# Local attention: one output product a step, with the three value terms added on GpSimd and VectorE

## The reference, cut to what matters

```python
q = (x @ WQ_w + WQ_b).reshape(Bx, Lx, nh, d)
k = (x @ WK_w + WK_b).reshape(Bx, Lx, nh, d)
ak = (ax @ WK_w + WK_b).reshape(Bx, 1, nh, d)
av = (ax @ WV_w + WV_b).reshape(Bx, 1, nh, d)
pad_k = jnp.pad(k, ((0, 0), (1, 1), (0, 0), (0, 0)))
k_shift = jnp.stack([pad_k[:, t:Lx + t] for t in range(3)], axis=3)
...
K = jnp.concatenate([akb, k_shift], axis=3)
V = jnp.concatenate([avb, k_shift], axis=3)
scores = jnp.einsum('blhd,blhjd->blhj', q, K) / jnp.sqrt(jnp.float32(d))
alphas = jax.nn.softmax(scores, axis=-1)
att = jnp.einsum('blhj,blhjd->blhd', alphas, V).reshape(Bx, Lx, nh * d)
return att @ WO_w + WO_b
```

## Time and profile before

| | us |
|---|---|
| median of 3 runs | 1583.0 |
| lowest and highest of them | 1581.71, 1587.13 |
| the profiled execution, its own time | 1581.07 |
| span of its trace | 1579.0 |
| TensorE busy, whole span | 1460.8 (93%) |
| VectorE busy | 732.8 (46%) |
| ScalarE busy | 651.0 (41%) |
| GpSimd busy | 106.7 (7%) |

### The profile page before, as it was taken

One profiled execution on the slowest core, in us unless ns is written; L12 is line 12 of the kernel. 1 busy time (PEld: TensorE's weight loads), 2 busy tenths in 40 slices (PEclk: granted clock), 3 DMA queues, 4 the chain that ended last, 5 costly groups with the idle time before them and its releaser, 6 DMA issues. The chain is left out here.

```text
span 1579.0 us, 30235 instructions
## 1 busy us (share of the span) xinstructions
PE 1460.8 (93%) x11078; PEld 1132.5 (72%) x11078; DVE 732.8 (46%) x2721; ACT 651.0 (41%) x2429; POOL 106.7 (7%) x141
## 2 busy tenths in 40 slices
PE   7999978999989999999999998799999999767995
PEld 5333324777779999999999996488888888644663
DVE  3576765455433444444444445633333332863223
ACT  2322204565524554554554552134444443622442
POOL 4000000000000000000000000100000000004662
PEclk8999989999999999999999998599999999957998
DMA  5000000000030000000000000100000000001113
GB/s 158 1 0 0 1 0 1 1 1 1 1 108 1 1 2 2 1 2 1 2 1 2 1 2 1 34 21 22 22 22 28 22 2 1 1 27 33 42 43 96
DMA packets 27724, 27.95 MB, mean 18 GB/s; under 512 B 2293, under 2 KB 22234, under 8 KB 27450
## 3 DMA queue, kind: packets, MB, share of 16 engines
q1 hardware_dynamic: 20970, 16.70, 3.6%
q0 software_dynamic: 2496, 5.12, 1.1%
q10 hardware_dynamic: 4112, 4.19, 0.9%
HBM read 21.35 MB, written 4.65 MB: 16 GB/s over the span
## 5 line engine op out<-in xcount | busy, mean ns | idle before, releaser
L1625 PE MATMUL spare<-identb 128*128 128x128 bf16 x3166 | 218.4, 219 | 0.0
L1625 PEld LDWEIGHTS spare<-identb 128*128 128x128 bf16 x3166 | 202.0, 103 | 4.3
L1223 DVE TENSOR_TENSOR_SCAN narg<-rz,pre_n 128x16 f32<-128x16 f32 x256 | 47.9, 187 | 220.2 <-PE pre_n L1120 219.0
L1158 ACT ACTIVATE ghid<-gh_ps,cols 128x128 f32<-128x128 f32 x512 | 144.3, 365 | 12.9 <-PE gh_ps L1059 12.7
L1059 PE MATMUL gh_ps<-hist,w 128*128 128x128 f32 x1024 | 137.5, 275 | 0.6 <-ACT ghid L1158 0.6
L1068 PE MATMUL gy_ps<-w2e,ghid 128*128 128x128 f32 x1024 | 136.8, 276 | 0.8 <-DVE g_diff L1204 0.3
L1068 PEld LDWEIGHTS gy_ps<-w2e,ghid 128*128 128x128 f32 x1024 | 124.4, 191 | 3.2 <-issue 3.2
L1059 PEld LDWEIGHTS gh_ps<-hist,w 128*128 128x128 f32 x1024 | 125.9, 188 | 0.8 <-DVE hist L1231 0.8
L1144 ACT ACTIVATE rz<-pre_r 128x8 f32<-128x8 f32 x256 | 45.6, 178 | 181.9 <-PE pre_r L1120 179.2
L1120 PE MATMUL pre_r<-hist,gru_w 128*128 128x128 f32 x512 | 118.1, 311 | 0.8 <-DVE hist L1231 0.5
L1676 DVE TENSOR_TENSOR_SCAN targ<-gates,pairs 128x16 f32<-128x16 f32 x256 | 49.1, 192 | 140.8 <-ACT gates L1635 140.8
(11 more groups left out here) (412 smaller groups left out, 2516.4 us busy)
## 6 DMA issues: line engine op xcount, KB each, us to landing
w<-in_L_ffn_W SPq DMA_DIRECT2D x1, 2048.0 KB, 9.6
raw<-in_L_ffn_wg SPq DMA_DIRECT2D x8, 256.0 KB, 3.0
raw<-in_L_ffn_wu SPq DMA_DIRECT2D x8, 256.0 KB, 2.8
raw<-in_L_ffn_wd SPq DMA_DIRECT2D x8, 256.0 KB, 2.7
wqkv<-in_L_attn_Wqkv SPq DMA_DIRECT2D x1, 1536.0 KB, 6.6
mrow<-mt SPq DMA_DIRECT2D x4, 256.0 KB, 2.4
y_top<-yrow SPq DMA_DIRECT2D x4, 256.0 KB, 5.4
y_next<-yrow ACTq DMA_DIRECT2D x4, 256.0 KB, 5.8
```

What stands on the lines that cost most here:

```text
L1158: nc.scalar.activation(hid[v % 2][:, f, :], h_ps[:, f, :], ACT.Relu, bias=n.cols[:, at:at + 1]).then_inc(h_done, 1)
L1223: V.tensor_tensor_scan(narg[p][:, :], rz[p][:, 0:16], n_slot(s), 0.0, ALU.mult, ALU.add).then_inc(narg_done, 1)
L1625: nc.tensor.matmul(spare[:, 0:P], n.identb[:, :], n.identb[:, :], start=True, stop=True)
```

## The change

The third term is no longer a product of its own: it is added to the pair sum, and one product with the sum of all three is left. The first addition moves from VectorE to GpSimd, and VectorE adds the third term one step later, between `weighted(u, 0)` and `weighted(u, 1)` of the next unit. A semaphore `all_done` is new. TensorE waits for it ahead of `project_out`. The number of additions on VectorE stays 32.

```diff
@@ block.gpsimd
+                def pair_terms(u):
+                    if not 0 <= u < STEPS:
+                        return
+                    pool.wait_ge(term_done, J * u + 2)
+                    if u >= 2:
+                        pool.wait_ge(y_part, u - 1)
+                    nc.gpsimd.tensor_tensor(pair[u % 2][:, :], term[u % 2][:, 0, :], term[u % 2][:, 1, :],
+                                            ALU.add).then_inc(pair_done, 1)
+
+                for u in range(STEPS):
+                    pair_terms(u)
@@ block.tensor, project_out
-                    pe.wait_ge(term_done, J * (u + 1))
-                    nc.tensor.matmul(y_ps[:, :], wo[:, c, :], term[u % 2][:, J - 1, :], start=False, stop=False)
-                    pe.wait_ge(pair_done, u + 1)
+                    pe.wait_ge(all_done, u + 1)
                     nc.tensor.matmul(y_ps[:, :], wo[:, c, :], pair[u % 2][:, :], start=False,
                                      stop=(c == NC - 1)).then_inc(y_part, 1)
@@ block.vector
                     if u >= 2 and j == 0:
-                        dve.wait_ge(y_part, u - 1)
+                        dve.wait_ge(pair_done, u - 1)
+                        dve.wait_ge(all_done, u - 1)
...
-                def pair_terms(u):
+                def all_terms(u):
                     if not 0 <= u < STEPS:
                         return
-                    dve.wait_ge(term_done, J * u + 2)
-                    nc.vector.tensor_tensor(pair[u % 2][:, :], term[u % 2][:, 0, :], term[u % 2][:, 1, :],
-                                            ALU.add).then_inc(pair_done, 1)
+                    dve.wait_ge(pair_done, u + 1)
+                    dve.wait_ge(term_done, J * (u + 1))
+                    nc.vector.tensor_tensor(pair[u % 2][:, :], pair[u % 2][:, :], term[u % 2][:, J - 1, :],
+                                            ALU.add).then_inc(all_done, 1)
...
                     weighted(u, 0)
+                    all_terms(u - 1)
                     if split:
                         soft_reciprocal(g)
                     weighted(u, 1)
...
                     if g is not None and at == 0:
                         soft_shift(g)
-                    pair_terms(u)
                     if split:
```

More of the change, by code:

```diff
@@ L232, in local_attention @@
         parts_done = sem("parts_done"); turned = sem("turned"); turned_kept = sem("turned_kept"); p0_kept = sem("p0_kept")
-        spread = sem("spread"); term_done = sem("term_done"); pair_done = sem("pair_done")
+        spread = sem("spread"); term_done = sem("term_done"); pair_done = sem("pair_done"); all_done = sem("all_done")
         y_part = sem("y_part"); y_kept = sem("y_kept")
```

## The result

The changed kernel took 1596.97 us in the median of 7 runs (1593.45 to 1603.44), the kernel before 1579.52 on the same chip (7 runs, 1575.41 to 1587.13). The ratio is 1.0109, with a 95% interval of 1.0081 to 1.0138: slower by about 17 us. The forecast was 1580.6, with a range from 1573 to 1587; it started from a median of 3 runs of the kernel before, 1583.0, that has become 1579.5 with 7, so its miss in the difference (2.4 less forecast, 17 more measured) is larger than the two times show. The profiled execution took 1594.89 us, its span is 1593.1.

What follows compares the result with a forecast made beforehand. TensorE set the 5.38 us step, the keys' ring limiting it to 5.12. Gains 6.4, less 1.9 (last steps) and 2.1 (softmax collisions), made 2.4 us less: 1583.0 to 1580.6 us, range 1573 to 1587.

Steps and rivals of the forecast that it cites:

- the nine steps of units 20 to 22 and 26 to 31: Steps without key projections and three-tap products: 3.43 us each against 3.22, 0.21 more each, a loss of 1.9 us.
- the ring: Last steps: third term, first term, second addition, product, third spread, back to third term; 3.43 us against 3.22.
- the 0.9 of the last group's first unit: Last group, where no keys and no product follow: the removed product's whole 0.86 us gained once.
- The clock rival: After each softmax TensorE idles 0.7 longer, 3.4 us more at 1.2 GHz: +5 us, 1585.7; 10 in 100.
- the 0.26 of unit 19: Unit 19, one of seven steady steps: each shrinks from 5.38 to 5.12 us, a gain of 0.26.
- The softmax collision: Steps 17, 25, 33: GpSimd's addition runs behind the three-tap product and delays VectorE's difference 0.7 each, 2.1 us lost.
- the steady step: Mid-group steps, units 3 to 5, 11 to 13 and 19: from 5.38 to 5.12 us, 1.8 us gained.
- the keys' ring: Third term, ScalarE's key copy, key projection, spread, second term, three-tap product, third term: 5.12 us, a step's lower limit.
- the addition's ring: Steady step: output product to next first term, second addition, back to the product; 5.09 us, just below 5.12.
- GpSimd's 1.28 alone: GpSimd's first addition: 1.28 us in the last steps, over 2 us where it lies behind a three-tap product.
- the rival at 1607: GpSimd takes the port ahead of the three-tap product in 20 steps, 1.2 us more each: +24 us; 10 in 100.
- the one at 1566: Keys' ring has slack and TensorE keeps the pace: some 20 steps gain 0.86 each, 17 us; 7 in 100.

Runs made afterwards that it cites:

- e2: Changed kernel plus one useless fp32 matmul of 512 columns a unit in units 20 to 31; 1585.2 us, ratio 1.0051 to the kernel before.
- e1: Kernel before with its third output product left out and nothing else changed; 1584.56 us, ratio 1.0027 to the kernel before.
- e4: Kernel before with its one addition moved to GpSimd and both output products kept; 1586.01 us, ratio 1.0035 to the kernel before.
- e8: Changed kernel with GpSimd held in units 7, 15 and 23 until the softmax's last cast; 1590.5 us, ratio 1.0060 to the kernel before.
- e9: The hybrid with a key ring of 13 slots instead of 12; 1573.29 us, ratio 0.9954 to the kernel before.
- the hybrid: Changed kernel in units 0 to 19, GpSimd held in units 7 and 15; two products and VectorE's old addition from unit 20; 1579.97 us, ratio 0.9977.
- e11: The hybrid without the hold on GpSimd in units 7 and 15; 1583.7 us, ratio 1.0013 to the kernel before.
- e7: Changed kernel plus one useless matmul of 256 columns a unit in units 20 to 31; 1587.2 us, ratio 1.0029 to the kernel before.
- e3: Changed kernel with the first addition back on VectorE in its old place; 1600.18 us, ratio 1.0131 to the kernel before.
- e10: e9 with the second addition moved ahead of the next unit's first term; 1571.21 us, ratio 0.9937 to the kernel before.
- e6: Changed kernel plus one useless matmul of 512 columns a unit in units 24 to 31 only; 1589.07 us, ratio 1.0042 to the kernel before.

## Why the prediction was wrong, by its steps

**The step that failed** is "I price the nine steps of units 20 to 22 and 26 to 31 with that, 0.21 each": 3.43 us a step, a loss of 1.9 us. The length was worked out at the 2.4 GHz level from rows of the kernel before, and the change took away what kept that level. In units 26 to 31 the step was 4.6 us. The excess of 1.17 is all in TensorE's two links of the ring: product to spreading 2.01 instead of 1.07, spreading to third term 0.65 instead of 0.41. With the clock brought back (e2) the same step is 3.42, so the ring was right and its clock was not. From unit 23 to the end of the stage that is +10.8 us, where the forecast has 6 x 0.21 = 1.3 less the 0.9 of the last group's first unit, so +0.4; the 1.8 us behind the stage come on top. e1 shows that one product a step less is enough for the loss, without the new waits. What I should have asked of the rows: TensorE is busy only 14.90 of 18 us in these steps before the change, the clock stood at 0.69 right behind a softmax with TensorE idle in it, and the change takes 0.86 us of work out of each of these steps with nothing to fill its place. I took the 1.00 of the row over as if it belonged to the place and not to the work.

**The clock rival** asked about the wrong place. It had 3.4 us more of the low level after each softmax, +5 us. That did happen after the second softmax (6.8 us instead of 3.4), but the large piece is that the clock did not return after the last one.

**Units 20 to 22** were mis-sized for a reason of their own, and the clock has no part in it: from unit 18 to 22 it was +2.96 instead of 3 x 0.21 = 0.6 less the 0.26 of unit 19, and e2, with the clock at 1.00 up to 209.9, takes the same 18.16 us. In steps 29 and 30 VectorE is the bound: the three-tap product, three terms and an addition are 1.67 + 4 x 0.61 = 4.11, and the step was 4.15 and 4.13. The product that closes a unit waits for that line. In step 33 the product of unit 22 stands behind the sum of the exponentials on VectorE as well, and TensorE waited 2.19 us for it. The rows of the changed kernel:

```profile
194.93 1.12 PE L411 MATMUL y_ps<-pair,wo 128*128 128x512 f32 x2 [0.86 <-DVE pair L654]
...
199.06 1.13 PE L411 MATMUL y_ps<-pair,wo 128*128 128x512 f32 x2 [0.88 <-DVE pair L654]
...
203.22 1.12 PE L411 MATMUL y_ps<-pair,wo 128*128 128x512 f32 x2 [1.17 <-DVE pair L654]
...
208.95 2.08 PE L411 MATMUL y_ps<-pair,wo 128*128 128x512 f32 x2 [2.19 <-DVE pair L654]
```

**The softmax collision** was taken as 0.7 "by the order of starts", with 0 and 1.28 as bounds. It is the upper bound's mechanism: GpSimd starts 0.03 after L612 and 0.24 ahead of the product, and the product is 1.08 longer. The order of starts was misread: the term ends at 112.47 and the product starts at 112.78, because two short operations stand between them, so by that order GpSimd comes first. In the steady step nothing stands between, and the product was ahead (89.22 against 89.38). In the last group there is no product and the cast takes it, 1.20 instead of 0.26. Together 3.1 us in place of 2.1 (e4, e8), and more where it lengthens the low clock.

**Right:** the steady step (5.1 forecast, 5.09 measured), with 0.61 us in front of the weights of the key projection put down to ScalarE's copy and at most 0.3 in front of the output product; the keys' ring of 5.12 (e1; "no further" was 0.03 too strict) and the addition's ring of 5.09 (e9) apart from one another; GpSimd's 1.28 alone and over 2 us behind a product (1.26, 2.72); no product but those in the softmax got longer. The gains up to unit 18, in the steps outside the softmax, were 4.64 us of a forecast 1.6 + 2.5 + 1.2 = 5.3 (six of the seven steady steps lie there). GpSimd ahead of the product in every step, the rival at 1607, did not happen; that TensorE keeps the pace, the one at 1566, neither, for the reason given.

By terms, in the order of the steps outside the softmax up to unit 18, the first two softmax steps, units 18 to 23, and the rest of the stage: forecast -5.3, +1.4, +1.1 and +0.4 make -2.4; measured -4.64, +2.55, +2.11 and +10.79 make +10.81.

## What to carry to other kernels

Before matmuls are taken out of a stretch in which TensorE already waits, look at what clock it is granted there and how dense its stream stays: a term of the sum that is priced at 2.4 GHz holds only if the work that is left is still granted it, so price such a stretch at 1.2 GHz as well. Take work away where TensorE is full and leave it where it is idle anyway, as the hybrid does (e11, 1.0013 against 1.0109). And an addition moved to GpSimd should be given its start by a wait that lies behind VectorE's critical operations, not be left to the order of starts (e8, 1.0060 against 1.0109).

## What the runs showed of the hardware that was not expected

- Less work for TensorE made a kernel slower (e1, 1.0027), and useless matmuls made one faster (e2, 1.0051 against 1.0109). The low level held for 58 us in the changed kernel though no single wait of a matmul in that stretch was over 2.2 us. With one fp32 product and three spreads in each of its steps the granted clock stayed at 0.50 to the end of the stage; with the fillers of e2 and e7 beside them it returned to 1.00. The Trainium skill, TensorE: Matmul & The Clock Gate, "A second HAM failure mode: psum-queue depth-cycling", tells of a kernel whose clock went down and up again because TensorE was idle for short times, and often, between groups of matmuls. By that rule this tail is at risk. The trace agrees in part: 8.2 us of waits for the addition in nine pieces, and the clock at 0.50, but it stayed there and did not go up and down.
- The clock also fell without a softmax's long wait: at 196.8 us in e3, with no wait of a matmul over 1.4 us in the 10 us before, and at 185.1 in e10, with none over 0.9 from 178 us on and TensorE busy 5.43 of the 7 us to 185.
- GpSimd slips in between two VectorE operations with two SBUF inputs that follow one another without a gap: 111.18 between 111.15 and the product that could only start at 111.42. The product, the cast and GpSimd's own addition show the exclusion in numbers: 2.83 against 1.75, 1.20 against 0.26, 2.72 against 1.26 us.
- The low stretches shift from one execution to the next by several us from the first steps on. The changed kernel, e2, e6 and e7 are the same up to unit 19, and yet their first copy of y_ps began at 127.1, 125.9, 128.5 and 129.6 us; e2 and e6 have a low stretch at 76.8 to 80.2 and 76.6 to 83.4 that the other two don't have. Two single profiles can't settle differences below some 4 us here.
